# Edge stage of a two-layer graph network: weight matrix keyed by half groups, another split of small work between VectorE and GpSimd

## The reference

```
h  = relu(layernorm(x))
m  = mish(mish([h[src], h[dst], edge_attr] @ W1 + b1) @ W2 + b2)     # a message for each edge
agg = segment_sum(m, dst)
x  = x + layernorm(h + mish([h, agg] @ W3 + b3) @ W4 + b4) * gamma + beta
h2 = relu(layernorm(x))
x  = x + relu(segment_sum((h2 @ U * s @ Vt)[src] * edge_weight, dst) + bias)
```

## Time and profile before

| | us |
|---|---|
| median of 3 runs | 1602.71 |
| profiled execution | 1601.37 |
| its span, first to last instruction | 1599.7 |
| TensorE busy | 1539.2 (96%) |
| VectorE busy | 1453.3 (91%) |
| ScalarE busy | 1307.5 (82%) |
| GpSimd busy | 1117.6 (70%) |

### The profile page before, as it was taken

The page is one execution under the profiler, slowest core; times in us unless marked ns, Lnnn a source line. Parts: engine busy times, 40 slices in busy tenths (PEclk is TensorE's granted clock), DMA queues, the critical chain, the costliest instruction groups (busy, mean ns, idle before and its releaser), DMA issues.

```text
span 1599.7 us, 32991 instructions
## 1 busy us (share of the span) xinstructions
PE 1539.2 (96%) x7870; PEld 1183.6 (74%) x7870; DVE 1453.3 (91%) x3139; ACT 1307.5 (82%) x2503; POOL 1117.6 (70%) x989
## 2 busy tenths in 40 slices
PE   6759999999999999999999999999999999999998
PEld 5537777777777777777777777777777777776785
DVE  6538999999999999999999999999999999995676
ACT  2218999989989999999999989899999999985462
POOL 3036788888888888878888888888888888862220
PEclk9879999999999999999999999999999999999999
DMA  8743444444445445445444444444444454455564
GB/s 297 258 148 99 118 119 115 124 112 121 120 110 125 121 107 130 117 109 125 117 113 120 118 112 121 117 115 119 118 115 123 112 122 121 108 138 127 119 141 158
DMA packets 109666, 205.08 MB, mean 128 GB/s; under 512 B 30377, under 2 KB 41001, under 8 KB 109632
## 3 DMA queue, kind: packets, MB, share of 16 engines
q0 software_dynamic: 48736, 119.55, 32.9%
q1 hardware_dynamic: 60896, 85.12, 17.0%
HBM read 151.52 MB, written 42.83 MB: 121 GB/s over the span
## 4 chain that ended last, share of the span: by engine, by line
PE 85%; DVE 5%; issue 2%; ACT 1%; DMA 0%; DVEq 0%; POOL 0%; ACTq 0%; POOLq 0%
PE bm L959 52%; PE bp L944 6%; PE bp L946 6%; PE bs L982 5%; PE bp L948 4%; PE pm L970 3%; PE pm L969 3%; PE pu L1836 1%; PE po L1858 1%; PE pu L330 1%; PE pu L1903 1%; DVE bm L1122 1%; PE pu L1890 0%; DVE rp L1094 0%; DVE tp L1103 0%
## 5 line engine op out<-in xcount | busy, mean ns | idle before, releaser
L874 POOL TENSOR_TENSOR hTl<-tp,hTh 128x512 fp32r<-128x512 f32 (+1 forms) x316 | 407.3, 1289 | 206.6 <-DVE kl L1131 196.6
L959 PE MATMUL bm<-W2h,hTh 128*128 128x512 f32 x1252 | 506.4, 404 | 2.6 <-DVE bm L1122 2.6
L959 PE MATMUL bm<-W2l,hTh 128*128 128x512 f32 x1252 | 495.3, 396 | 0.0
L959 PE MATMUL bm<-W2h,hTl 128*128 128x512 f32 x1252 | 495.0, 395 | 0.0
L857 POOL DMA_INDIRECT xg<-A_tab,idx x309 | 327.9, 1061 | 61.2 <-issue 54.3
L959 PEld LDWEIGHTS bm<-W2h,hTh 128*128 128x128 f32 x1252 | 235.1, 188 | 90.0 <-DVE bm L1122 24.4
L959 PEld LDWEIGHTS bm<-W2l,hTh 128*128 128x128 f32 x1252 | 235.3, 188 | 56.7
L959 PEld LDWEIGHTS bm<-W2h,hTl 128*128 128x128 f32 x1252 | 235.5, 188 | 49.2
L1094 DVE SCALAR_TENSOR_TENSOR rp<-rp 128x512 f32<-128x512 f32 (+1 forms) x316 | 239.1, 757 | 27.6 <-ACT rp L1015 27.1
L1015 ACT ACTIVATE rp<-bp 128x512 f32<-128x512 f32 (+1 forms) x316 | 186.0, 589 | 80.9 <-PE bp L948 76.5
L1018 ACT ACTIVATE rp<-rp 128x512 f32<-128x512 f32 (+1 forms) x316 | 196.8, 623 | 48.9 <-DVE rp L1094 48.9
(11 more groups left out here) (217 smaller groups left out, 2453.0 us busy)
## 6 DMA issues: line engine op xcount, KB each, us to landing
ea<-in_eaT SPq DMA_DIRECT2D x156, 128.0 KB
M_tab<-mev POOLq DMA_DIRECT2D x79, 160.0 KB
agg_tab<-ev POOLq DMA_DIRECT2D x157, 64.0 KB
db<-in_dst_rows SPq DMA_DIRECT2D x78, 128.0 KB
M<-M SPq DMA_DIRECT2D x78, 128.0 KB
M_tab<-zero POOLq DMA_DIRECT2D x10, 640.0 KB, 21.2
eaW<-Bh_tab SPq DMA_DIRECT2D x79, 64.0 KB
eaW<-Bl_tab SPq DMA_DIRECT2D x79, 64.0 KB
```

The source lines that it names most:

```text
L874: e.tensor_tensor(hTl[p][:, j, 0:w], tp[u.const % 2][:, 0:w], hTh[p][:, j, 0:w], ALU.subtract)\
L959: last = e.matmul(bank[0:r, :], a[p][:, c, j * P:j * P + r], w[:, c, :], start=False, stop=c == KC - 1 and w is W2l, skip_group_check=True)
```

## The change

- The sources are cut into eight parts of 160 (EQ, EC) instead of four of 320, and the window of destinations is 16 nodes (EWIN) instead of 32, with a base of its own for each half group of 256 edges. The keys are still 128. The two halves write into two column ranges of `pm`, 0 to 159 and 160 to 319, and M_tab gets one adding transfer for each half.
- kh and kl become one tile khl, written by one scalar_tensor_tensor over 2 x 128 columns, with broadcast operands.
- The low part of ea is made by VectorE (`prep`, k = 2, six slots ahead), no longer by GpSimd (seven slots ahead).
- GpSimd issues one gather in every slot, the last one a slot later than before, and one adding transfer in every slot: agg_tab in j1 and j3, M_tab in j2 and j0.
- Before the loop, the windows of half groups are found, the program takes the narrow path only if each half group stays within 16 nodes, and the part of a source is found by a multiply and a shift.

```diff
-KEYS = Q * WIN
+EQ = 8
+EC = NP // EQ
+EWIN = 16
+KEYS = EQ * EWIN
+HSUB = SUB // 2
...
-                        c_v.inc(e.tensor_reduce(win[:, 0:1], dsti[:, :], AX.X, ALU.min))
-                        link(e.tensor_reduce(mx[:], dsti[:, :], AX.X, ALU.max))
+                        halves = dsti[:, :].rearrange("g (h n) -> g h n", h=2)
+                        c_v.inc(e.tensor_reduce(win[:, 2:4], halves, AX.X, ALU.min))
+                        link(e.tensor_reduce(mx[:], halves, AX.X, ALU.max))
+                        c_v.inc(e.tensor_reduce(span[:, 2:3], mx[:], AX.X, ALU.max))
+                        link(e.tensor_scalar(win[:, 2:4], win[:, 2:4], float(NP - EWIN), None, ALU.min))
+                        c_v.inc(e.scalar_tensor_tensor(span[:, 0:2], mx[:], float(WIN - EWIN), win[:, 2:4], ALU.add, ALU.subtract))
+                        link(e.tensor_reduce(win[:, 0:1], win[:, 2:4], AX.X, ALU.min))
...
-                        link(e.tensor_scalar(rem[:], scolf[:], float(QC), None, ALU.is_ge))
-                        for r in range(2, Q):
-                            link(e.scalar_tensor_tensor(rem[:], scolf[:], float(r * QC), rem[:], ALU.is_ge, ALU.add))
+                        link(e.tensor_scalar(scoli[:], scolf[:], float(-(-2 ** 19 // EC)), None, ALU.mult))
+                        link(e.tensor_scalar(scoli[:], scoli[:], 19, None, ALU.arith_shift_right))
+                        link(e.tensor_copy(rem[:], scoli[:]))
...
-    PREP_AHEAD = (9, 8)
-    LOW_EA_AHEAD = 7
-    GATHER_AHEAD = {2: (10, (0,)), 3: (9, (1,)), 0: (8, (2, 3))}
+    PREP_AHEAD = (9, 8, 6)
+    GATHER_AHEAD = {2: (10, (0,)), 3: (9, (1,)), 0: (8, (2,)), 1: (7, (3,))}
+    ADJ_LAG = {2: (6, 0), 0: (8, 1)}
...
-                    wait(e, g_prep, u.group(1, -1))
+                    wait(e, s_ealow, u.group(1, -1))
...
-            def adjacency(u, b):
-
-                e.wait_ge(a_adj, u.group(1, 1))
-                wait(e, q_adj, u.group(16))
-                e.dma_start(M_d[bass.ds(b * Q, KEYS), :], mev[u.par][:], accum_op=ALU.add).then_inc(q_adj, 16)
+            def adjacency(u, half):
+
+                b = e.value_load(base_i[0:1, bass.ds(u.group(3, 1 + half), 1)], min_val=0, max_val=NP - EWIN)
+                if half == 0:
+                    e.wait_ge(a_adj, u.group(1, 1))
+                wait(e, q_adj, u.group(32, 16 * half))
+                if half:
+                    e.sem_inc(s_go, 1)
+                e.dma_start(M_d[bass.ds(b * EQ, KEYS), :], mev[u.par][:, half * EC:(half + 1) * EC], accum_op=ALU.add)\
+                 .then_inc(q_adj, 16)
...
-                g = s + LOW_EA_AHEAD
-                if g.j == 0 and g.has(4 * NG):
-                    low_ea(g)
...
-                e.wait_ge(v_adj, u.val(3, 3))
-                e.matmul(pm[:, 0:QC], kh[i][0:r, :], so[i][0:r, :], start=u.j == 0, stop=False, skip_group_check=True)
-                e.matmul(pm[:, 0:QC], kl[i][0:r, :], so[i][0:r, :], start=False, stop=u.j == SUB - 1 or tail(u),
+                e.wait_ge(v_adj, u.val(2, 2))
+                e.matmul(half, khl[i][0:r, 0, :], so[i][0:r, :], start=u.j % HSUB == 0, stop=False, skip_group_check=True)
+                e.matmul(half, khl[i][0:r, 1, :], so[i][0:r, :], start=False, stop=u.j % HSUB == HSUB - 1 or tail(u),
                          skip_group_check=True).then_inc(s_adj, 1)
...
+                elif k == 2:
+                    e.wait_ge(s_prep, u.group(2, 1))
+                    e.tensor_tensor(M2[p][0:64, 0:n], ea[p][0:64, 0:n], M2[p][0:64, 0:n], ALU.subtract)\
+                     .then_inc(s_ealow, 1)
...
-                e.tensor_scalar(so[i][0:r, :], iota_q[0:r, :], scol4[0:r, c], None, ALU.is_equal).then_inc(v_adj, 1)
-                e.tensor_scalar(kh[i][0:r, :], iota_k[0:r, :], kcol[0:r, c], wcol_h[0:r, c].bitcast(F32), ALU.is_equal,
-                                ALU.mult).then_inc(v_adj, 1)
-                e.tensor_scalar(kl[i][0:r, :], iota_k[0:r, :], kcol[0:r, c], wcol_l[0:r, c], ALU.is_equal, ALU.mult)\
-                 .then_inc(v_adj, 1)
+                e.tensor_scalar(so[i][0:r, :], iota_q[0:r, :], scol8[0:r, c], None, ALU.is_equal).then_inc(v_adj, 1)
+                e.scalar_tensor_tensor(khl[i][0:r, :, :],
+                                       iota_k[0:r, :].rearrange("p (a k) -> p a k", a=1).to_broadcast([r, 2, KEYS]),
+                                       kcol[0:r, c],
+                                       wcol_hl[0:r, c, :].rearrange("p a (h k) -> p (a h) k", k=1).bitcast(F32)
+                                       .to_broadcast([r, 2, KEYS]), ALU.is_equal, ALU.mult).then_inc(v_adj, 1)
...
-                for k in range(2):
+                for k in range(3):
```

More of the change, by code:

```diff
@@ L243, in gnn_two_layers @@
     Sl_d = dram("Sl_tab", (NP, R))
-    win_d = dram("win_tab", (NG, 2))
-    M_d = dram("M_tab", (NP * Q, QC))
+    win_d = dram("win_tab", (NG, 4))
+    M_d = dram("M_tab", (NP * EQ, EC))
     with ctx:
@@ L267, in gnn_two_layers @@
         ev = [sb(f"ev{i}", [2 * WIN, H]) for i in range(2)]
-        mev = [sb(f"mev{i}", [KEYS, QC]) for i in range(2)]
+        mev = [sb(f"mev{i}", [KEYS, 2 * EC]) for i in range(2)]
         st, sb_early, _ = scope()
@@ L377, in gnn_two_layers @@
             wcol = sb1("wcol", [P, NG * SUB])
[L378 to L379 removed]
+            win = sb1("win", [NG, 4])
+            mx = sb1("mx", [NG, 2])
+            span = sb1("span", [NG, 3])
             far = sb1("far", [1, 4])
             iota_i = sb1("iota_i", [P, WIN], I32)
[L382 removed]
+            iota_qi = sb1("iota_qi", [P, EC], I32)
             iop_i = sb1("iop_i", [P, 1], I32)
@@ L772, in edge_narrow @@
         oh = [sb(f"oh{i}", [P, SUB, WIN]) for i in range(2)]
-        so = [sb(f"so{i}", [P, QC], F32R) for i in range(2)]
-        kh = [sb(f"kh{i}", [P, KEYS], F32R) for i in range(2)]
-        kl = [sb(f"kl{i}", [P, KEYS], F32R) for i in range(2)]
+        so = [sb(f"so{i}", [P, EC], F32R) for i in range(2)]
+        khl = [sb(f"khl{i}", [P, 2, KEYS], F32R) for i in range(2)]
         bp = [ps(f"bp{i}") for i in range(2)]
@@ L859, in gather @@
                      .then_inc(q_ga[p], 16)
-            def low_ea(u):
-                p, n = u.par, ETAIL if tail(u) else G
-                e.wait_ge(s_prep, u.group(2, 2))
-                e.tensor_tensor(M2[p][0:64, 0:n], ea[p][0:64, 0:n], M2[p][0:64, 0:n], ALU.subtract).then_inc(g_prep, 1)
             def low(u):
@@ L877, in base @@
             def base(u):
-                return e.value_load(base_i[0:1, bass.ds(u.group(), 1)], min_val=0, max_val=NP - WIN)
+                return e.value_load(base_i[0:1, bass.ds(u.group(3), 1)], min_val=0, max_val=NP - WIN)
             def accumulate(u, a, b):
@@ L916, in step @@
                     accumulate(q, 0, held[0])
-                if q.j == 2 and q.has(4 * FULL):
-                    adjacency(q, held[0])
+                if s.j in ADJ_LAG:
+                    lag, half = ADJ_LAG[s.j]
+                    if (s + -lag).has(4 * FULL):
+                        if half == 0 and s.reg is None and s.const == lag:
+                            e.wait_ge(q_z, 16 * (ZERO_DMAS + NCH))
+                        adjacency(s + -lag, half)
                 if q.j == 3 and q.has(4 * FULL):
@@ L925, in _ @@
             accumulate(At(None, 4 * FULL), 0, held[0])
-            adjacency(At(None, 4 * FULL), held[0])
+            adjacency(At(None, 4 * FULL), 0)
             e.wait_ge(q_acc, 16 * (ACCS * FULL + 1))
-            e.wait_ge(q_adj, 16 * NG)
+            e.wait_ge(q_adj, 16 * (2 * FULL + 1))
             e.sem_inc(s_agg, 1)
@@ L940, in pre @@
                     e.wait_ge(q_win[p], u.pair(48, 48))
-                    e.wait_ge(g_prep, u.group(1, 1))
+                    e.wait_ge(s_ealow, u.group(1, 1))
                 for t in range(SUB if w == G else 1):
@@ L1042, in adjacency @@
                 e.wait_ge(s_adj, u.val(1, 1 if tail(u) else SUB))
-                wait(e, q_adj, u.group(16, -16))
-                e.activation(mev[u.par][:], pm[:, 0:QC], ACT.Copy).then_inc(a_adj, 1)
+                wait(e, q_adj, u.group(32, -32))
+                n = EC if tail(u) else 2 * EC
+                e.activation(mev[u.par][:, 0:n], pm[:, 0:n], ACT.Copy).then_inc(a_adj, 1)
             def evac(u):
```

52 lines of the change are left out of this document (29 added, 23 removed).

## The result

| | before | after |
|---|---|---|
| median | 1603.57 (4 runs) | 1575.39 (4 runs, 1575.13 to 1575.43) |
| profiled span | 1599.7 | 1573.8 |
| first segment sum starts | 153.7 | 153.1 |
| last segment sum starts | 1462.1 | 1435.5 |

The kernel before has one run more here than ahead of the prediction. The ratio to before is 0.9824, 95% interval 0.9807 to 0.9841: 28 us faster, 1.8%. All of it lies inside the edge loop: between the first and the last segment sum 1308.4 us became 1282.4, and what comes ahead and behind changed by under 1 us each.

A forecast was written before the change was run, and what follows sets the result against it. TensorE was taken to bound the kernel, VectorE nearly full too. 17.0 - 0.58 + 0.10 + 0.07 = 16.59 us a group, 0.41 saved times 78, +1 before the loop: 1572 us; forecast 1560 to 1582, range 1553 to 1597.

The forecast's parts named there:

- TensorE's pair: The two adjacency products of a slot, now 160 columns each: 0.15 us instead of 0.29, saving 0.58 us a group.
- rival (1): Weight loads partly pace the short adjacency products: 0.22 us a pair, 15 us saved, about 1587 us; chance 0.14.
- Bias waits: TensorE's wait for VectorE's bias copy at the messages of j1: grows from 0.09 to about 0.19 us a group.
- VectorE: VectorE's busy time a group: 16.74 - 0.77 + 0.61 - 0.22 = 16.36 us, level with TensorE's 16.37.
- The bound of 0.80 for khl: Upper bound on VectorE's merged key operation, from the one-hot with broadcast inputs: 0.80 us, a loss of 0.13 a slot.
- the one-hot's 0.40: VectorE's 128-column one-hot with broadcast inputs lasts 0.40 us, explained by GpSimd's hTl running, without any price for broadcasting.
- The hold: VectorE's in-place square in j1, held up by GpSimd's subtract for ea: 0.22 us a group, which goes.
- The last gather: xg part 3, issued 2.0 us later: TensorE waits before j3's transposes, 0 to 0.7 us a group, taken as 0.07.
- Rival (3): The gather of xg part 3 exceeds 4.0 us from issue to start: group 17.2 us, +16, about 1618; chance 0.10.
- GpSimd's load: GpSimd's queue in a group: the subtract goes (1.24 us), one M_tab issue comes (1.04), so the load is level.
- the narrow path: The guard asks for 256 edges within 16 nodes; they cover about 8 to 10, so the path stays.
- Before the loop: Six short window operations and one key pass more, less three passes that made the quarter: at most +1 us.

The follow-up runs named there:

- without the low product: The changed kernel without the second of each slot's two adjacency products, so the low part of the weights is left out: 1576.30 us, ratio 0.9818 to before.
- the keys alone: The changed kernel with the low part of ea back on GpSimd in j1 and both last gathers in j0, as before: 1608.18 us, ratio 1.0027 to before.
- the one with the gathers first: The changed kernel with each slot's gather issued ahead of hTl instead of behind it: 1568.18 us, ratio 0.9775 to before.

## Why the prediction was right, and where its terms were off

The forecast was 1572 us, the median is 1575.4; the group was to be 16.59 us and is 16.66. That the sum came out so near is in part luck, for three of its terms were off and cancel. Summed over the starts of TensorE's timeline from 200 to 1390 us, a group lost 0.33 us: 0.34 by the pair and not 0.58; 0.10 by bias waits that went, where 0.10 more was forecast; 0.14 was given back in front of the transposes of j3, where 0.07 was forecast; some hundredths came from the other matmuls.

- **TensorE's pair** (0.58 a group saved): mis-sized, it measured 0.34. The pair was to take 0.15; it takes 0.19, and the transposes behind it 0.33 instead of 0.29 or 0.30. In the three slots followed by transposes that is 0.59 - 0.51 = 0.08 each, in j2 0.11: 0.34 a group. The price is that of rival (1), 0.22 a pair and 0.3 a group, which I gave 0.14, and its mechanism, weight loads that set the pace of the short products, fits what the runs show. The row that I relied on, the transposes at 73 ns, has loads that last 141 ns on the page's groups, against 187 to 190 for all other loads of 128 columns; I had taken them for the same load. Why they are shorter stays open. The figure that the Trainium skill gives for such a load ("TensorE: Matmul & The Clock Gate", "LDWEIGHTS (loading the stationary operand)"), 107 ns, agrees with the 0.11 us measured here.
- **Bias waits** (+0.10): wrong in sign. They were to grow from 0.09 to 0.19 in j1 and are nearly gone (2.80 to 2.82 in all slots; the total of that wait fell from 14.1 to 8.6 us). The step that failed is "TensorE comes to the messages of j1 two pairs earlier (0.29)": counted from the segment sum it comes only 0.11 earlier (9.79 and 9.68, medians), since the pairs give less and the wait for the gather gives some back, and the bias copy comes 0.21 earlier (9.06 and 8.85). Cheaper products bring the wait back: without the low product the messages of j1 take 2.91. So one error fed the other.
- **VectorE**: right in the terms it had. so 0.21, khl 0.40, low part of ea 0.60 a step, the square of j1 back at 0.68; busy 16.22 a group against 16.36 forecast (for two changes it had no term: the steps of the cast hTh fell by 0.19 a group, those of tp rose by 0.13). The bound of 0.80 for khl with broadcast inputs was far off; the one-hot's 0.40 was a hold, as I had argued: it ends when hTl has ended, and lasts 0.71 where hTl starts later beside it.
- **The hold** (0.22 saved): right for the step from before to after, but too small for what the subtract would have cost once j0 has one more transfer: 1.2 to 1.4 us in the two versions that left it on GpSimd. I had read 0.22 as its price; it was the price at one place. The Trainium skill's rule ("SBUF — State Buffer", "Who interferes with whom") that a VectorE instruction with two SBUF inputs and a GpSimd instruction that reads SBUF exclude each other agrees with the runs: the square ends 0.56 to 0.57 us after the subtract in the kernel before, with the keys alone, and with the low part of ea on GpSimd.
- **The last gather** (+0.07): the right wait at half its size, 0.14. The usual groups lose 0.06 to 0.07 (the step of 1.06 instead of 1.00), which the table of waits leaves out; it lists 5.2 us between 200 and 1400 us, another 0.07 a group. Nearly all of that lies in seven groups, six of them 200 us apart (354.4, 555.6 and so on to 1355.8). In those one GpSimd issue comes 0.66 late, as here (M_tab transfer, hTl and last gather; then TensorE's transposes, 0.48 idle):

```profile
549.61 0.95 POOL L908 DMA_DIRECT2D M_tab<-mev  x1 [0.66 <-issue]
550.25 1.67 POOL L883 TENSOR_TENSOR hTl<-tp,hTh 128x512 fp32r<-128x512 f32 x1
552.08 1.06 POOL L872 DMA_INDIRECT xg<-A_tab,idx  x1 [0.16 <-issue]
```
```profile
555.61 0.53 PE L959 MATMUL bp<-ident_r,xg 128*128 128x128 f32 x4 [0.48 <-issue]
```

The usual group waits so little because the 3.7 us from issue to use are just what the gather takes. What lies behind GpSimd's pause every 200 us stays open.
- **Rival (3)** was the right thing to fear: issue to use is 3.7 us, and the point from which it would have turned the change into a loss was given as 4.0. The run without the low product and the one with the gathers first show that this loop holds the changed kernel at nearly the same period as TensorE's own work.
- **GpSimd's load** "level" and **the narrow path** stays: right (busy 651 and 644 us of 800). **Before the loop** "at most +1 us": the first segment sum starts 0.6 us earlier, so the 1 us in the sum was not there.

## What to carry to other kernels

Give a stall of an engine its price at the place where the new order puts it: the same subtract held the same square for 0.2 us before and for 1.4 us when one more transfer came ahead of it, and two edits that each lose on their own gained 1.8% together. When an edit of the engine that seems to pace gives nothing, look for a second loop of the same period, here a gather that is issued behind an instruction that waits; issuing it ahead of that instruction gained 8 us, and an edit that had given nothing then gave 15. Don't price a matmul of few columns by its columns: with 128 columns of fresh weights it cost 0.11 us here wherever it stood, where its 160 columns alone were priced at 0.077, and the transposes at 0.073 were no guide to it. When a wait is too short for the table of waits, compare the steps from start to start over all groups.

## What the runs showed of the hardware

- A product of 160 columns with a fresh load of 128x128 costs TensorE 0.11 us, 0.07 for itself and 0.035 on the matmul behind it; single loads of 128 columns start 0.10 to 0.11 us apart at the closest, though each record lasts 0.19. The loads of the transposed gather rows last 141 ns and allow 0.073 to 0.083 each.
- VectorE's scalar_tensor_tensor with both tensor inputs broadcast over 256 columns takes 0.47 us; the rows of 316 and 512 columns gave an estimate of 0.48.
- With the keys alone, VectorE's in-place square waited 1.4 us for a GpSimd subtract, and that subtract lasted 1.74 us in place of 1.30; why it lasted longer isn't shown.
- VectorE's one-hot (two inputs, 128 columns) ended 0.15 to 0.17 us after GpSimd's hTl in the groups looked at, whether that made it 0.40 or 0.71 us long.
- An indirect gather of 128 rows of 2 KB needs 3.7 us from the start of its issue to the first matmul that uses it.
